# Differential attention in a four-layer decoder: four-tile passes with the keys in partitions in place of single tiles with the queries in partitions

## The reference

```python
q1 = _split_heads(query @ q1_w.T, B, Nq)
q2 = _split_heads(query @ q2_w.T, B, Nq)
attn1 = jax.nn.softmax(jnp.einsum('bhqd,bhkd->bhqk', q1, k1) * SCALE, axis=-1)
attn2 = jax.nn.softmax(jnp.einsum('bhqd,bhkd->bhqk', q2, k2) * SCALE, axis=-1)
lambda_full = lambda_1 - lambda_2 + LAMBDA_INIT
diff_attn = attn1 - lambda_full * attn2
x = jnp.einsum('bhqk,bhkd->bhqd', diff_attn, v1)
x = x.transpose(0, 2, 1, 3).reshape(B, Nq, C)
xf = x.astype(jnp.float32)
xf = xf * jax.lax.rsqrt(jnp.mean(xf * xf, axis=-1, keepdims=True) + EPS) * norm_w
return x @ proj_w.T + proj_b
```

## Time and profile before

| | us |
|---|---|
| median of three runs | 1149.68 |
| lowest and highest | 1148.88, 1149.77 |
| span of the profiled execution | 1167.4 |
| busy in it: PE, DVE, ACT, POOL | 956.1, 619.4, 559.0, 399.0 |

### The profile page before, as it was taken

The page is one execution under the profiler, slowest core; times in us unless marked ns, Lnnn a source line. Parts: engine busy times, 40 slices in busy tenths (PEclk is TensorE's granted clock), DMA queues, the critical chain, the costliest instruction groups (busy, mean ns, idle before and its releaser), DMA issues. The chain is left out here.

```text
span 1167.4 us, 20624 instructions
## 1 busy us (share of the span) xinstructions
PE 956.1 (82%) x7766; PEld 805.2 (69%) x7766; DVE 619.4 (53%) x1699; ACT 559.0 (48%) x1069; POOL 399.0 (34%) x394
## 2 busy tenths in 40 slices
PE   4888999999988999979888783999367875299992
PEld 3566899999976999846666562989145554288882
DVE  7876412111266343578787653444498763444443
ACT  2666644343446334357665531656245542155552
POOL 4545110000043001500110434547365555545552
PEclk9999999999998999989998875989689985599996
DMA  9999900000000000000000004655200001445543
GB/s 349 183 179 185 199 26 2 1 1 1 1 2 1 1 1 1 1 1 2 1 2 1 28 18 136 201 175 165 73 1 1 1 10 32 137 154 168 170 153 109
DMA packets 70578, 83.83 MB, mean 72 GB/s; under 512 B 5298, under 2 KB 57529, under 8 KB 70353
## 3 DMA queue, kind: packets, MB, share of 16 engines
q1 hardware_dynamic: 64336, 71.98, 26.4%
q0 software_dynamic: 4992, 8.45, 2.1%
q10 hardware_dynamic: 1152, 2.10, 0.5%
HBM read 52.15 MB, written 32.18 MB: 72 GB/s over the span
## 5 line engine op out<-in xcount | busy, mean ns | idle before, releaser
L2374 ACT ACTIVATE hT<-PS,par 128x512 f32<-128x512 f32 x200 | 136.4, 688 | 174.3 <-PE PS L2278 172.8
L2414 DVE SCALAR_TENSOR_TENSOR X<-PS,wts,X 128x128 f32<-128x128 f32 x272 | 76.5, 345 | 218.3 <-PE PS L2297 218.3
L1105 ACT ACTIVATE hT<-PS 116x512 f32<-116x512 f32 (+1 forms) x192 | 102.5, 561 | 108.0 <-PE PS L863 99.4
L863 PE MATMUL PS<-par,score 128*116 128x128 f32 x704 | 114.8, 303 | 23.3 <-DVE oc L1007 12.5
L2297 PEld LDWEIGHTS PS<-regA,hT 128*128 128x128 f32 x1024 | 119.1, 192 | 3.1 <-issue 0.5
L2297 PE MATMUL PS<-regA,hT 128*128 128x128 f32 x1024 | 119.5, 275 | 0.0
L863 PEld LDWEIGHTS PS<-par,score 128*116 128x116 f32 x704 | 85.2, 149 | 41.0 <-issue 31.9
L1179 POOL TENSOR_TENSOR score<-score,mx 128x1232 f32<-128x1232 f32 x32 | 72.0, 2251 | 90.3 <-DVE mx L987 90.3
L2045 PE MATMUL PS<-q_up,halves 128*112 128x256 f32 (+1 forms) x276 | 85.6, 310 | 8.8 <-DVE hT L2154 8.8
L2276 PE MATMUL PS<-x_up,w_halves 128*128 128x512 f32 x200 | 86.4, 432 | 0.2 <-ACT hT L2374 0.2
L1082 ACT ACTIVATE score<-score 128x1232 f32<-128x1232 f32 x64 | 78.3, 1223 | 10.1 <-POOL score L1179 10.1
(11 more groups left out here) (315 smaller groups left out, 2016.2 us busy)
## 6 DMA issues: line engine op xcount, KB each, us to landing
regA<-L3f_w SPq DMA_DIRECT2D x23, 704.0 KB
regB<-L2f_w SPq DMA_DIRECT2D x23, 578.0 KB
L2f_sorted_x<-empty_row SPq DMA_DIRECT2D x8, 1161.0 KB, 21.0
L3f_sorted_x<-empty_row SPq DMA_DIRECT2D x8, 1161.0 KB, 20.2
regA<-L0f_w SPq DMA_DIRECT2D x4, 768.0 KB, 16.9
regA<-L2f_sorted_x SPq DMA_DIRECT2D x23, 129.0 KB, 3.8
regB<-L3f_sorted_x SPq DMA_DIRECT2D x23, 129.0 KB, 4.1
par<-params SPq DMA_DIRECT2D x1, 2450.0 KB, 13.8
```

Source lines behind the costliest of these rows:

```text
L863: last = nc.tensor.transpose(PS[0:BW, bank_of(("exps", 3 * u + i)), (j % 4) * P:(j % 4) * P + P], exps_of(u)[:, first:first + BW], ident)
L1105: nc.scalar.activation(hT[0:BW, u % 2, i, 0:width], PS[0:BW, bank, 0:width], ACT.Copy).then_inc(pT_ready.sem, 1)
L2374: nc.scalar.activation(hT[:, n % 2, k, :], PS[:, i % 4, :], c["act"], bias=pc(f"{tag}_b1")[:, col:col + 1]).then_inc(h_ready.sem, 1)
```

## The change

L2x gets a stage of its own, `wide_stage`. A pass is one batch (512 tokens) with one set of queries and keys, so there are 8 passes, and each has 3 steps, since four heads x 77 keys = 308 rows are cut into 103, 103 and 102 partitions. In a step the product has the keys in the partitions and 512 tokens in the free dimension, one bank for each group of four heads. The shift by the maximum is a fourth matmul: the maxima of a tile are still computed with the queries in the partitions (the old scores, in eight pieces of two banks a pass), written as upper and lower halves into rows, transposed (`turn`) and copied to shiftT. The exponentials go from PSUM to hT and are used as they lie: `values` with head-masked values (vwide) and `sums` with a 0/1 matrix give, for 128 output dimensions in the partitions, the weighted values and the sum of each head repeated for its 8 dimensions. `divide` takes the reciprocal of 128x512 on VectorE. The square sums come from a matmul with a column of ones, the projection uses the attended values as weights, and the last scaling and addition to X are one operation. The norm weight is multiplied into the projection's weights and the bias is added to X, both on POOL. The L2f routing gets groups of 4, 4, 4, 4 tiles, parts of 8, 4, 4, and new due steps: statistics 8, 14, 20, 26; apply 9, 15, 21; rows 10, 16, 22; logits 11, 17, 23; read 12, 18, 24; choose 18, 24; second 19, 25; ranks 20, 26; place 21. The key preparation moves unchanged into `key_stage`; the value preparation of L2x becomes three matmuls and three masked copies; `lead`'s projections of groups 2 and 3 stand between the first maxima. The core of the diff:

```diff
...
+            def pairs(i, ps):
+                return [("max", 8 * i + p) for p in ps] if i < passes else []
+            def finished(i):
+                return i // 2 - 1 if i >= 2 and i % 2 == 0 else None
+            def extras(n):
+                i, k = divmod(n, 3)
+                b = finished(i)
+                parts = [[], [], []]
+                if k == 0:
+                    parts[0] += pairs(i + 1, (2,))
+                    parts[1] += pairs(i + 1, (3,))
+                if k == 1:
+                    parts[0] += pairs(i + 1, (4, 5))
+                    parts[1] += pairs(i + 1, (6,))
+                    parts[2] += pairs(i + 1, (7,))
+                    if b is not None:
+                        parts[2].append(("ss", b))
+                if k == 2:
+                    if i + 1 < passes:
+                        parts[0].append(("turn", i + 1))
+                    if b is not None:
+                        parts[0].append(("y", b))
+                    parts[1] += pairs(i + 2, (0,))
+                    parts[2] += pairs(i + 2, (1,))
...
+            head = [("max", p) for p in range(8)] + [("turn", 0)] + [("max", 8), ("max", 9)]
+            banks = {"max": (4, 5), "turn": (4,), "ss": (5,), "y": (5,), "rows": (4,), "logits": (5,), "ranks": (4,)}
+            freed = {"max": (max_read, 1), "turn": (shift_ready, 1), "ss": (ss_read, 1), "y": (x_done, TG),
...
+                def maxima(u):
+                    i, p = divmod(u, 8)
+                    (b, s), (j, h) = divmod(i, sets), divmod(p, 2)
+                    t = TG * b + j
+                    for m, (half, u_k) in enumerate(((up, 0), (up, 1), (low, 0))):
+                        for r in (2 * h, 2 * h + 1):
+                            dims = slice(32 * r, 32 * r + 32)
+                            last = nc.tensor.matmul(PS[:, 4 + r % 2, 0:HR * K], half[dims, t * P:t * P + P], kb[dims, s, u_k, b, :, :],
+                                                    start=m == 0, stop=m == 2)
+                    last.then_inc(max_psum.sem, 1)
+                def turn(i):
+                    pe.wait_ge(rows_ready.sem, rows_ready.at(TG * (i + 1)))
+                    for j in range(TG):
+                        last = nc.tensor.transpose(PS[:, 4, j * P:j * P + P], max_rows[:, j, :, :].rearrange("p g c -> p (g c)"), ident)
+                    last.then_inc(turn_psum.sem, 1)
+                def products(n):
+                    i, k = divmod(n, 3)
+                    b, s = divmod(i, sets)
+                    up, low = q[s]
...
+                    if n:
+                        pe.wait_ge(exp_ready.sem, exp_ready.at(n))
+                    for m, (half, u_k) in enumerate(((up, 0), (up, 1), (low, 0))):
+                        for r in range(RG):
+                            dims = slice(32 * r, 32 * r + 32)
+                            nc.tensor.matmul(PS[0:w, r, :], kb[dims, s, u_k, b, :, :].rearrange("p h k -> p (h k)")[:, at:at + w], half[dims, cols],
+                                             start=m == 0, stop=False)
+                    if k == 0:
+                        pe.wait_ge(shift_ready.sem, shift_ready.at(i + 1))
+                    for r in range(RG):
+                        dims = slice(32 * r, 32 * r + 32)
+                        last = nc.tensor.matmul(PS[0:w, r, :], minus_head[dims, at:at + w], shiftT[dims, :], start=False, stop=True)
+                    last.then_inc(prod_ready.sem, 1)
+                def values(n):
+                    i, k = divmod(n, 3)
+                    if k == 0 and i:
+                        pe.wait_ge(sums_used.sem, sums_used.at(i))
+                    pe.wait_ge(exp_ready.sem, exp_ready.at(n + 1))
+                    w = WIDE[k]
+                    for r in range(RG):
+                        nc.tensor.matmul(PS[32 * r:32 * r + 32, 6, :], vwide[0:w, k, i // sets, r, :], hT[0:w, n % 2, r, :],
+                                         start=k == 0, stop=k == 2)
+                def sums(n):
+                    k = n % 3
+                    w = WIDE[k]
+                    for r in range(RG):
+                        last = nc.tensor.matmul(PS[32 * r:32 * r + 32, 7, :], pc("head_cols", w)[:, 32 * k:32 * k + 32], hT[0:w, n % 2, r, :],
+                                                start=k == 0, stop=k == 2)
+                    last.then_inc(sums_psum.sem, 1)
+                def square_sums(b):
+                    pe.wait_ge(sq_ready.sem, sq_ready.at(b + 1))
+                    for j in range(TG):
+                        last = nc.tensor.matmul(PS[:, 5, j:j + 1], w_sq[:, j * P:j * P + P], pc("ones")[:, 0:1], start=True, stop=True)
+                    last.then_inc(ss_psum.sem, 1)
...
+                    for j in range(TG):
+                        last = nc.tensor.matmul(PS[:, 5, j * P:j * P + P], w_att[:, j * P:j * P + P], pc("L2x_wo"), start=True, stop=True)
...
+                for n in range(steps + 3):
+                    first, middle, end = extras(n)
+                    if n < steps:
+                        products(n)
+                    for use in first:
+                        do(use)
+                    if 0 < n <= steps:
+                        values(n - 1)
+                    for use in middle:
+                        do(use)
+                    if 0 < n <= steps:
+                        sums(n - 1)
+                    for use in end:
+                        do(use)
+            def vector(v, st):
+                def maxima(u):
...
+                    v.wait_ge(max_psum.sem, max_psum.at(u + 1))
+                    ps = PS[:, 4:6, 0:HR * K].rearrange("p r (h k) -> p r h k", h=HR)
+                    nc.vector.tensor_reduce(m[:, 8 * h:8 * h + 8].rearrange("p (r h) -> p r h", r=2), ps, AX.X, ALU.max).then_inc(max_read.sem, 1)
+                    if h == 0:
+                        return
+                    v.wait_ge(max_read.sem, max_read.at(u + 1))
...
+                    nc.vector.tensor_copy(up.bitcast(F32R), m).then_inc(v_step, st.one())
+                    v.wait_ge(v_step, st.n)
+                    nc.vector.tensor_tensor(max_rows[:, j, :, HR:2 * HR], m, up, ALU.subtract).then_inc(rows_ready.sem, 1)
+                def divide(i):
+                    s = i % sets
+                    v.wait_ge(sums_psum.sem, sums_psum.at(3 * (i + 1)))
+                    nc.vector.reciprocal(w_rec, PS[:, 7, :]).then_inc(v_step, st.one())
+                    v.wait_ge(v_step, st.n)
+                    if s == 0:
+                        nc.vector.tensor_tensor(w_first, PS[:, 6, :], w_rec, ALU.mult).then_inc(sums_used.sem, 1)
+                    else:
+                        nc.vector.scalar_tensor_tensor(w_second, PS[:, 6, :], lam[:, 0:1], w_rec, ALU.mult, ALU.mult).then_inc(sums_used.sem, 1)
+                def correct(i):
+                    b, s = divmod(i, sets)
+                    if s == 0:
+                        return
...
+                    nc.vector.tensor_tensor(w_att, w_first, w_second, ALU.subtract).then_inc(att_ready.sem, 1)
+                    v.wait_ge(att_ready.sem, att_ready.at(b + 1))
+                    nc.vector.tensor_tensor(w_sq, w_att, w_att, ALU.mult).then_inc(sq_ready.sem, 1)
...
+                    nc.vector.tensor_scalar(oss[:, :], PS[:, 5, 0:TG], 1.0 / D, RMS_EPS, ALU.mult, ALU.add).then_inc(ss_read.sem, 1)
...
+                        nc.vector.scalar_tensor_tensor(X[:, t, :], PS[:, 5, j * P:j * P + P], osr[:, j:j + 1], X[:, t, :], ALU.mult, ALU.add)\
+                            .then_inc(x_done.sem, 1)
...
+                    b = finished(i)
+                    route["vector_step_first"](v, st, n, bank_of)
+                    if k == 0:
+                        maxima(8 * (i + 1) + 2)
+                        maxima(8 * (i + 1) + 3)
+                    if k == 1:
+                        maxima(8 * (i + 1) + 4)
+                        if i:
+                            divide(i - 1)
+                        maxima(8 * (i + 1) + 5)
+                        if i:
+                            correct(i - 1)
+                        maxima(8 * (i + 1) + 6)
+                        maxima(8 * (i + 1) + 7)
+                        if b is not None:
+                            mean_squares(b)
+                    if k == 2:
+                        if b is not None:
+                            finish(b)
+                        maxima(8 * (i + 2))
+                        maxima(8 * (i + 2) + 1)
+                    route["vector_step"](v, st, n)
+                def exps(n, h):
+                    w = WIDE[n % 3]
+                    a.wait_ge(prod_ready.sem, prod_ready.at(n + 1))
+                    if n >= 2:
+                        a.wait_ge(sums_psum.sem, sums_psum.at(n - 1))
+                    ins = nc.scalar.activation(hT[0:w, n % 2, 2 * h:2 * h + 2, :], PS[0:w, 2 * h:2 * h + 2, :], ACT.Exp, scale=scale)
+                    ins.then_inc(*((exp_ready.sem, 1) if h else (a_step, st.one())))
```

(30 more changed lines are left out.)

411 lines of the change are left out of this document (255 added, 156 removed).

## The result

The changed kernel took 1212.28 us (median of four runs, 1209.86 to 1221.23); the kernel before, run beside it, 1149.72. The ratio is 1.0564 [1.0525, 1.0603]: slower, as forecast, but by 62.6 us where the forecast said 14.

The account below looks back on a forecast made before the run. It took PE and DVE, working in turn without slack, as the stage's bound. Head, passes, routing and end summed to 229.7 us from 500.3, reaching 730.0 against 715.9: +14.1, so 1164 us, range 1140 to 1195.

Parts of the forecast that it names:

- the round trip of a piece: Maxima pieces share one bank pair, so each takes 0.15 + 0.75 + 0.80 = 1.70 us between PE and DVE.
- the division standing ahead of the values: In step 1, 4.1 us on DVE holds the values matmuls and piece 6; PE idles 3.6 us.
- the late groups: Late routing after the last X: 16 scatters wait, 25.4 against 18.4 us before, 7 of the loss.
- Rival B: Long reciprocal costs like any 512-column operation: seven divisions lose 2.6 us each, so 1145.5 us; chance 0.10.
- E: Four matmuls of 32 output columns do not run side by side: +2.6 us twice a step, near 1290; chance 0.03.
- C: Pieces do not bind and the stage runs at DVE's busy time: 1104 us, half of it 1134; chance 0.12.
- the sum: Case A, all stage terms added: 229.7 us, last scatter 730.0 against 715.9, slower at 1164 us; chance 0.50.
- The walk: Steady pass followed job by job on PE and DVE: 20.8 us for an odd pass, 23.7 for an even one.
- rival D: Clock stays low through the new passes after PE's idle gaps: 5 us more a pass, 1194 us; chance 0.25.
- the cover: POOL's bias additions and extra key set-up hide while DVE and PE do the norms: 0, or 2 us if not.
- POOL's queue: At pass 7's end, 16 scatters hold the last batch's power of -1/2: 24.3 us to last X, otherwise about 21.
- no pieces, 3.35 a step: Pass 7 has no maxima pieces, so each step costs only PE's and ACT's own work, 3.35 us.

Follow-up runs that it names:

- the kernel with filled waits: Changed kernel with idle 128x128 matmuls put into PE's waits (before values, pieces 6 and 7, later head pieces); ratio 1.0503 to the kernel before.
- the moved piece: Kernel with the division in quarters, with maxima piece 4 moved to the end of step 0; ratio 1.0277 to the kernel before.
- groups 1, 2 and 4: Sets of follow-up runs on chips where the kernel before took 1170.8, 1171.1 and 1173.2 us.
- group 3: Set of follow-up runs on a chip where the kernel before took 1149.5 us; the unchanged changed kernel had ratio 1.0529 there.

## Why the prediction was wrong in size

Point by point, in the order of its sum. The last scatter came 43.2 us later than predicted (730.0 to 773.2):

| term | predicted | measured | more |
|---|---|---|---|
| start of pass 0 | 522.5 | 531.0 | 8.5 |
| pass 0 | 16 | 21.3 | 5.3 |
| passes 1 to 6 with routing | 141.8 | 165.9 | 24.1 |
| pass 7 to last X | 24.3 | 29.3 | 5.0 |
| last X to last scatter | 25.4 | 25.7 | 0.3 |

The timed result is 48.3 us above the forecast. Behind the last scatter after is 12.4 us shorter than before (439.1 for 451.5), and the 17.7 us by which the profiled execution of before was longer than its timed runs, taken off in the forecast, don't recur in after: 43.2 - 12.4 + 17.7 = 48.5.

**What held.** The prices of the new operations; the round trip of a piece at the full clock (1.63 for 1.70); the division standing ahead of the values (PE idle 3.3 for 3.6, and 2.67 us a pass by the copy in its place); matmuls of 32 output columns side by side (1.06 for four of 512 columns); the late groups (7.6 for 7 in their place). Rival B is out by the row of 3349 ns, E by 1.06 us. C, pieces that do not bind, is out: without 56 of them the kernel is 68.6 us shorter.

**What failed, first: the clock, as a term of the sum.** The walk granted the low clock to values, piece 6, sums and piece 7 of a step 1, and full clock to all the rest, the head and pass 0 included. But the head fell to 1.2 GHz at 505.8 and stayed there to 549.6 (granted 0.50 over the whole stretch), through pass 0. This is rival D, which was priced for six passes and not for the rest. The head's 8.5 us are worked out from rows like these:

```profile
501.56 2.53 DVE L572 TENSOR_SCALAR xn<-X,mv,rstd 128x128 f32<-128x128 f32 x4
...
507.41 3.75 PE L714 MATMUL PS<-xnT,par 128*128 128x512 f32 x4 [0.78 <-ACT xnT L674]
...
519.13 0.80 DVE L1023 TENSOR_REDUCE mx<-PS 128x8 f32<-128x616 f32 x1 [2.37 <-PE PS L907]
...
521.21 0.80 DVE L1023 TENSOR_REDUCE mx<-PS 128x8 f32<-128x616 f32 x1 [1.28 <-PE PS L907]
```

Two projections of four records at 3.75 where the earlier trace rows give 1.8, 4 us; eight pieces 2.08 apart instead of 1.70, 3 us; and the norm of the last group beside POOL's bias addition, 2.53 where the earlier trace rows give 1.11, 1.4 us. That last one was the cover that I costed at nothing, with 2 us if it failed. It failed. Another 1.0 us was there ahead of the stage: its first scores start at 501.30 and not at 500.29. These four make 9.4 for 8.5, so a part of them is hidden.

**What failed, second: the jobs that wait behind a piece.** The products of the passes start at 552.1, 574.1, 601.4, 630.0, 659.6 and 688.2, those of pass 7 at 718.0. So an odd pass without routing took 21.9 (said 20.8), and the low clock behind its division was priced well: products of step 2 start 11.3 us into step 1 (said 11.4). In pass 2 they start 15.2 us into it. The square sums wait until piece 7 has been read, and the products, which ran beside piece 7 in pass 1, now stand behind them: 3.9 us, for which the sum had 1.5. In pass 3 the row transposes do the same:

```profile
620.67 1.12 PE L1922 MATMUL PS<-par,regA 128*128 128x128 f32 x4 [0.90 <-DVE mx L1023]
621.72 1.18 PE L927 MATMUL PS<-q_up,kb 32*102 32x512 f32 x8
...
629.04 1.06 PE L1929 MATMUL PS<-par,xnT 128*128 128x8 f32 x8 [0.89 <-DVE mx L1023]
```

There the products start 14.4 us into step 1: 3.1 more than in pass 1, and the sum had 1.0. Put together, the 24.1 us are 6.8 in what all six passes have (21.9 for 20.8), 7.4 in what the even passes add, and 9.8 in the routing, which took 18.1 where the sum had 8.3.

**How much of this is the clock?** In the kernel with filled waits the granted clock is 1.00 through passes 1, 3 and 5, and they still take 21.0, 26.0 and 26.0 (21.9, 28.7 and 28.6 in after; said 20.8, 24.7 and 24.7). So in an odd pass of after the low clock costs 1 to 2.7 us, more by what the fillers themselves cost (and 4.6 in pass 1 of its second execution, which took 25.6), and routing still costs 5.0 where the sum had 3.9. Over six passes the fillers bought back 11 us, 1.9 a pass, less what they cost themselves. D's price of 5 us a pass is not borne out as a mean, and its 1194 would have been too low all the same, by 18 us. The low clock of the even passes, in their steps 0 too, stands in rows like these:

```profile
632.00:638.50 6.50, 6.50 (x44) 2.84 (x36) 1.60 (x4) 1.46 (x3) 0.00 (x0) 0.50 0.00 0
690.00:696.50 6.50, 6.50 (x42) 2.59 (x36) 2.77 (x9) 1.35 (x3) 0.00 (x0) 0.50 0.00 0
```

I gave D 0.25 and the sum 0.50, though the only row of a comparable gap, already showed 0.66 after waits shorter than the new ones. "Steps 0 and 2 are dense" was the argument against D; these two rows refute it: both begin in a step 0, and PE is busy without a break at 0.50. The Trainium skill, "TensorE: Matmul & The Clock Gate", section on the clock gate, calls the throttled state the default, and the trace agrees: 90 of 166 us.

Clock and waits can't be parted fully by these runs. The division moved off PE's path took 13.7 us of waiting at the same clock; the moved piece took 12.4 us of PE's busy time and 2.9 of its waiting; and differences of 5 us stand between executions of one kernel.

**A wrong step: POOL's queue.** I let the 16 scatters hold the last power. They were through 3.4 us earlier, so the DVE and PE chain set the end, and that chain was 29.3 and not 21. I had counted "no pieces, 3.35 a step" and forgotten that pass 7's first values still wait for pass 6's division: step 1 of pass 7 took 8.6 us (721.2 to 729.9), part of it at 1.2 GHz. With fewer pieces, in the kernel with quarters and maxima of pass 0 alone, POOL's power does start right behind the last of the scatters (644.90 + 0.96, then 645.88). The mechanism was right for that kernel and hidden in this one.

**The gain that the edit could bring.** Steps without pieces were put at 24 x 3.35 = 80 us. The run with no shift has 2.99 in its dense steps and 4.5 on the mean of passes 1 to 6. So the gain was real, and the maxima, which the change computes beside the new products, used it up: with the division in quarters both times, the ratio is 1.0424 with them and 0.9559 without.

## What to carry to other kernels

An edit that takes work off the engines can lose when what is left is joined by more round trips: 64 small pieces, each a hand-over from PE to DVE and back over one pair of banks, cost 1.2 us each although the maximum itself takes 0.80. Where a change adds waits to PE, price the lower clock for the stretches before and behind the new waits too, and not only for the instructions next to them. And price a small job that waits behind a piece by what it holds up: its own time and the overlap that the next products lose. And before moving a costly operation out of the way, ask whether it is needed: the shift by the maximum was worth 8% of the kernel here (ratio 1.0424 with it, 0.9559 without, both with the division in quarters), and these inputs did not need it.

## What the runs showed of the hardware

- **Clock.** In after the granted clock was 0.50 for stretches of 6.5 to 14 us in passes 1 to 6 and for 44 us in the head, although PE was busy 78% (34.1 of 43.8 us) in that one. Most of them begin in or just behind a wait of PE of 2.8 us or more. But the two at 632.0 and 690.0 begin where PE had last stood 0.9 us, and in the kernel with the copy, where it stands 1.08 us at most in these passes, the clock is 0.74 all the same. So a long wait is not the only way there.
- **Reciprocal.** 3.349 us for 512 elements, 0.934 for 128: 6.3 ns an element, as the slope of rows of 4 and 16 elements said. The Trainium skill, "VectorE: DVE Perf Modes", section "First, the fixed hardware budget", gives a repeat count of 8, by which I had 4.4; the measurement says about six steps of 1.04 ns.
- **VectorE beside GpSimd.** The norm over SBUF took 0.63 an operation instead of 0.28 while POOL added the bias.
- **Stalls during indirect scatters on some chips.** Where before takes 1171 and not 1149.5, VectorE and ScalarE stand while POOL scatters. The waits of VectorE in the run with no shift, 600 to 800 us (us in total, times, longest):

```profile
DVE logits_of L1985 <- remote: 16.0, 1, 16.0
```

The logits were ready at 613.7 and were read at 627.6, 1.3 us after the last of the 16 scatters; no engine's record explains the wait. The same wait (13 to 21 us) stands in the trace of every kernel with the new stage in groups 1, 2 and 4, and in none of group 3, nor in that of after. From pass 7 to the last scatter it takes 61 to 65 us where it is seen and 51 to 55 where it is not. The profiled execution of before has waits of this kind, 18.0 us in all on VectorE and ScalarE and up to 4.5 us each, and that of after has none. That is the likely reason why the span of before lay 17.7 us above its median and why the spans differ by less than the times; since the waits can overlap, it is not shown. What holds the engines there was not tried.
